# Row scores of the first attention as pairs of 64-row products, with queries and keys from float32r parts

## The reference, cut to what matters

```python
h = _layernorm(x, axis=-1) * (1 + ca) + sa
# _L0_attn_ref, H = 8 heads, R = 64 wide for queries and keys, values 128 wide
Q = (x @ Wq.T).reshape(b, n, H, R)
K = (x @ Wk.T).reshape(b, n, H, R)
V = (x @ Wv.T).reshape(b, n, H, d)
attn = jnp.einsum('bnhr,bmhr->bhnm', Q, K)
attn = jax.nn.softmax(attn, axis=-1)
out = jnp.einsum('bhnm,bmhd->bnd', attn, V)
```

## Time and profile before

| what | us |
|---|---|
| median of 3 runs | 3644.22 (3643.92 to 3647.78) |
| the profiled execution | 3644.25 |
| its span, first to last instruction | 3642.5 |
| attention, by the chain of its heads | about 35 to 1985 |
| TensorE busy in 1000 to 2000 us | 993.50 |
| VectorE busy in 1000 to 2000 us | 620.02 |
| ScalarE busy in 1000 to 2000 us | 491.84 |

### The profile page before, as it was taken

One profiled execution on the slowest core, in us unless ns is written; L12 is line 12 of the kernel. 1 busy time (PEld: TensorE's weight loads), 2 busy tenths in 40 slices (PEclk: granted clock), 3 DMA queues, 4 the chain that ended last, 5 costly groups with the idle time before them and its releaser, 6 DMA issues. The chain is left out here.

```text
span 3642.5 us, 82462 instructions
## 1 busy us (share of the span) xinstructions
PE 2897.9 (80%) x32284; PEld 2387.4 (66%) x32284; DVE 2611.7 (72%) x8488; ACT 1316.9 (36%) x2231; POOL 236.5 (6%) x155
## 2 busy tenths in 40 slices
PE   5999999999999999999999465656565666654455
PEld 2888888888888888888888344545454444442222
DVE  4565766756657566566664699999999999946775
ACT  2544454544444545454544022222222222211222
POOL 0000000000000000000000010000000000002220
PEclk9999999999999999999999666767676766766777
DMA  1000000000000000000000200000000000000000
GB/s 63 1 1 7 1 1 7 1 2 7 1 7 1 1 7 1 7 1 1 7 1 1 91 1 0 0 0 0 0 0 0 0 0 0 0 6 10 12 12 17
DMA packets 6415, 25.26 MB, mean 7 GB/s; under 512 B 1360, under 2 KB 1872, under 8 KB 5840
## 3 DMA queue, kind: packets, MB, share of 16 engines
q1 hardware_dynamic: 6224, 22.57, 1.6%
HBM read 14.18 MB, written 8.39 MB: 6 GB/s over the span
## 5 line engine op out<-in xcount | busy, mean ns | idle before, releaser
L605 PEld LDWEIGHTS obank<-v_one,probs 128*128 128x128 f32 x8192 | 1069.2, 190 | 91.1 <-issue 2.1
L605 PE MATMUL obank<-v_one,probs 128*128 128x129 f32 x8192 | 1078.6, 274 | 0.0
L352 ACT ACTIVATE probs<-bank 128x512 f32<-128x512 f32 x1024 | 583.8, 597 | 746.6 <-PE bank L593 450.2
L442 DVE TENSOR_REDUCE maxes<-ring 128x1 f32<-128x512 f32 x1024 | 659.7, 686 | 128.8 <-PE ring L573 105.6
L592 PE MATMUL bank<-q_hh,k_hl 128*128 128x512 f32 x1024 | 505.1, 493 | 1.6 <-issue 1.4
L593 PE MATMUL bank<-q_lm,k_h 65*128 65x512 f32 x1024 | 406.4, 397 | 0.0
L455 DVE RECIPROCAL recip<-obank 128x1 f32<-128x1 f32 x512 | 83.6, 163 | 414.2 <-PE obank L605 401.0
L573 PE MATMUL ring<-k_hl,q_hh 128*128 128x512 f32 x1024 | 338.4, 410 | 9.9 <-DVE k_hl L434 6.0
L1017 PE MATMUL ring<-ident_sb,to_turn 128*128 128x128 f32 x96 | 28.7, 437 | 365.7 <-ACT to_turn L855 359.7
L954 DVE TENSOR_TENSOR low_hot<-ids,low_iota 128x16384 f16<-128x16384 f16 x32 | 277.9, 8683 | 1.8 <-ACT ids L860 1.8
L1017 PEld LDWEIGHTS ring<-ident_sb,to_turn 128*128 128x128 f32 x96 | 16.1, 213 | 369.7 <-issue 340.3
(11 more groups left out here) (220 smaller groups left out, 3677.1 us busy)
## 6 DMA issues: line engine op xcount, KB each, us to landing
xt<-in_x SPq DMA_DIRECT2D x8, 512.0 KB, 8.6
out_x<-xt SPq DMA_DIRECT2D x8, 512.0 KB, 2.6
x<-out_x SPq DMA_DIRECT2D x1, 4096.0 KB, 12.0
out_x<-x SPq DMA_DIRECT2D x8, 512.0 KB, 2.6
pk_wq<-in_w_q SPq DMA_DIRECT2D x1, 1024.0 KB, 4.9
pk_wqT<-in_w_qT SPq DMA_DIRECT2D x1, 1024.0 KB, 7.1
wmod_sb<-in_wmod SPq DMA_DIRECT2D x2, 384.0 KB
w_qk_sb<-in_w_qk SPq DMA_DIRECT2D x1, 512.0 KB, 4.5
```

What stands on the lines that cost most here:

```text
L352: nc.scalar.activation(probs[:, half, i, :], st[s % 4], ACT.Exp).then_inc(st_free[s % 4], 1)
L442: nc.vector.tensor_reduce(maxes[:, i, k:k + 1], ring[bank_of(at)][:], AX.X, ALU.max).then_inc(rows_maxed, 1)
L605: mm = nc.tensor.matmul(obank[j % 2][:, 0:D + 1], probs[:, half, m, cols], v_one[h % 2][:, m, :], start=(m == 0), stop=(m == TB - 1))
```

## The change

It does three things.

1. Row scores. `k_top` is a new tile whose rows 64 to 127 hold the keys' float32r part. The product of key half 0 uses rows 0 to 63 of q_hh and k_hl; that of key half 1 uses rows 64 to 127 of q_hh and k_top. Both are 64-row products, on the two row halves of the array. The remainder of the keys is left out of the maxima (it stays in the scores that are exponentiated). Both banks are taken ahead of the first of the two.
2. ScalarE makes one more copy of 64x512 for each token half, into k_top, and VectorE and POOL wait for four copies instead of three.
3. Queries and keys come from three float32r products in place of a float32 one. The weights are split into two parts once; h is split for each batch by one more ScalarE copy and a VectorE subtraction for each half (`fine_h`, in slot 14 of head 6), and TensorE's q_and_k waits for that.

```diff
@@ ScalarE: turned_h and q_and_k
                 for k in range(2):
                     at = located(b, "t", ahead, k)
                     wait_full(b, at)
+                    nc.scalar.activation(hT_h[:, k * HALF:(k + 1) * HALF], ring[bank_of(at)][:], ACT.Copy).then_inc(hT_h_ready, 1)
                     nc.scalar.activation(hT[:, k * HALF:(k + 1) * HALF], ring[bank_of(at)][:], ACT.Copy).then_inc(hT_ready, 1)
...
                     nc.scalar.activation(q_hh[s][R:P, cols], bank[0:R, :], ACT.Copy).then_inc(hi_ready, 1)
+                    nc.scalar.activation(k_top[s][R:P, cols], bank[R:P, :], ACT.Copy).then_inc(hi_ready, 1)
@@ VectorE: q_and_k, the new fine_h, its place, and the start-up
-                    dve.wait_ge(hi_ready, 6 * g + 3 * k + 3)
+                    dve.wait_ge(hi_ready, 8 * g + 4 * k + 4)
...
+            def fine_h(b, ahead):
+                for k in range(2):
+                    cols = slice(k * HALF, (k + 1) * HALF)
+                    dve.wait_ge(hT_h_ready, 2 * (b + ahead) + k + 1)
+                    dve.wait_ge(hT_ready, 2 * (b + ahead) + k + 1)
+                    nc.vector.tensor_tensor(hT_l[:, cols], ring[bank_of(located(b, "t", ahead, k))][:], hT_h[:, cols].bitcast(F32), ALU.subtract).then_inc(hT_l_ready, 1)
...
+                        if s == 14 and h == H - 2 and not last:
+                            fine_h(b, 1)
...
+            link(nc.vector.tensor_copy(w_qk_h[:], w_qk_sb[:]))
+            nc.vector.tensor_tensor(w_qk_l[:], w_qk_sb[:], w_qk_h[:].bitcast(F32), ALU.subtract).then_inc(w_split, 1)
             dve.wait_ge(first_x_loaded, 16)
             for n in range(8):
                 first_norm(link, n, 0, 1)
+            fine_h(0, 0)
@@ TensorE: q_and_k and score_rows
-                pe.wait_ge(hT_ready, 2 * batch + 3)
+                pe.wait_ge(hT_l_ready, 2 * batch + 3)
                 for k in range(2):
                     at = located(b, "p", h, k)
-                    bank = take(b, at)
-                    give(at, nc.tensor.matmul(bank[:], w_qk_sb[:, h % H, :], hT[:, k * HALF:(k + 1) * HALF], start=True, stop=True))
+                    bank, cols = take(b, at), slice(k * HALF, (k + 1) * HALF)
+                    nc.tensor.matmul(bank[:], w_qk_l[:, h % H, :], hT_h[:, cols], start=True, stop=False)
+                    nc.tensor.matmul(bank[:], w_qk_h[:, h % H, :], hT_l[:, cols], start=False, stop=False)
+                    give(at, nc.tensor.matmul(bank[:], w_qk_h[:, h % H, :], hT_h[:, cols], start=False, stop=True))
...
-                for k in range(2):
-                    at = located(b, "a", h, i, k)
-                    bank = take(b, at)
-                    give(at, nc.tensor.matmul(bank[:], q_hh[s][:, i * P:(i + 1) * P], k_hl[s][:, k * HALF:(k + 1) * HALF], start=True, stop=True))
+                banks_ = [take(b, located(b, "a", h, i, k)) for k in range(2)]
+                for k, keys in enumerate((k_hl[s], k_top[s])):
+                    rows = slice(k * R, (k + 1) * R)
+                    give(located(b, "a", h, i, k),
+                         nc.tensor.matmul(banks_[k][:], q_hh[s][rows, i * P:(i + 1) * P], keys[rows, k * HALF:(k + 1) * HALF], start=True, stop=True))
```

More of the change, by code:

```diff
@@ L157, in build_attention @@
         k_hl = [sb(f"k_hl{i}", [P, N], F32R) for i in range(2)]
+        k_top = [sb(f"k_top{i}", [P, N], F32R) for i in range(2)]
+        w_qk_h = sb("w_qk_h", [P, H, 2 * R], F32R)
+        w_qk_l = sb("w_qk_l", [P, H, 2 * R], F32R)
+        hT_h = sb("hT_h", [P, N], F32R)
+        hT_l = sb("hT_l", [P, N], F32R)
         k_h1 = [sb(f"k_h1{i}", [R + 1, N], F32R) for i in range(2)]
@@ L174, in build_attention @@
         hT_ready = sem("hT_ready")
+        hT_h_ready = sem("hT_h_ready")
+        hT_l_ready = sem("hT_l_ready")
         ring_full = [sem(f"ring_full{r}") for r in range(2)]
@@ L190, in build_attention @@
         consts = sem("attn_consts")
+        w_split = sem("w_split")
         steps = sem("attn_steps")
         turns = sem("turns")
-        primed = [hT_ready, lo_ready, v_ready, rows_maxed, neg_ready, *st_free, *o_read]
+        primed = [hT_l_ready, lo_ready, v_ready, rows_maxed, neg_ready, *st_free, *o_read]
         def iteration_uses(b, h):
@@ L237, in released @@
             if kind == "t":
-                return hT_ready, shift(b, 2 * n + uses[at][2] + 1, 2)
+                return hT_l_ready, shift(b, 2 * n + uses[at][2] + 1, 2)
             if kind == "p":
@@ L285, in second_k @@
             def second_k(g, h):
-                pool.wait_ge(hi_ready, 6 * g + 6)
+                pool.wait_ge(hi_ready, 8 * g + 8)
                 if not (isinstance(g, int) and g < 2):
@@ L529, in _ @@
             pe.wait_ge(consts, 5)
+            pe.wait_ge(w_split, 1)
             def take(b, at):
@@ L550, in q_and_k @@
             def q_and_k(b, h, batch):
-                pe.wait_ge(hT_ready, 2 * batch + 3)
+                pe.wait_ge(hT_l_ready, 2 * batch + 3)
                 for k in range(2):
                     at = located(b, "p", h, k)
-                    bank = take(b, at)
-                    give(at, nc.tensor.matmul(bank[:], w_qk_sb[:, h % H, :], hT[:, k * HALF:(k + 1) * HALF], start=True, stop=True))
+                    bank, cols = take(b, at), slice(k * HALF, (k + 1) * HALF)
+                    nc.tensor.matmul(bank[:], w_qk_l[:, h % H, :], hT_h[:, cols], start=True, stop=False)
+                    nc.tensor.matmul(bank[:], w_qk_h[:, h % H, :], hT_l[:, cols], start=False, stop=False)
+                    give(at, nc.tensor.matmul(bank[:], w_qk_h[:, h % H, :], hT_h[:, cols], start=False, stop=True))
             def v_of(b, h):
+                pe.wait_ge(hT_ready, 2 * (b + h // H) + 2)
                 for k in range(2):
```

## The result

| kernel | median us | runs | profiled execution's span |
|---|---|---|---|
| before | 3644.68 | 4 (3643.92 to 3647.78) | 3642.5 |
| changed | 3823.73 | 4 (3820.5 to 3825.47) | 3823.5 |

The changed kernel is slower: its ratio to the kernel before is 1.0487, 95% interval 1.0472 to 1.0503, some 179 us. The forecast was 3800, range 3732 to 3858.

A forecast was written before the change was run, and what follows sets the result against it. TensorE's order of work was taken to set the pace, with a chain across three engines arriving together with it. Heads 135.5, h 9.9, start-up 9.0 and head 0's loop 1.5 add 155.9 to 3644.2: 3800 us, range 3732 to 3858.

The forecast's parts named there:

- The switches: Row-score slots on TensorE: two changes between 128 and 64 rows per slot, 0.20 us each, making the slot 2.00 us.
- The pair's overlap: Row scores on TensorE: the two 64-row products overlap, taking 0.235 us in place of 0.47.
- Both banks first: Row-score slots: the next pair waits until both banks are reduced, a second floor of 1.87 to 1.88 us, under 2.00.
- The chain: From q_and_k through ScalarE's copies and VectorE's subtractions to a head's first row scores: 1.23 - 0.15 - 0.06 = +1.02 us.
- The parts: q_and_k as float32r products: TensorE's time falls from 1.72 to 1.41 us, but TensorE then idles some 1.3 us.
- A head: One q_and_k to the next in attention: 1.02 + 1.17 - 0.04 = 2.15 us more, 63 times, 135.5 us.
- The split of h: Copies and subtractions of h once a batch delay q_and_k by 1.4 us, seven times: +9.9 us.
- The start-up: Before the regular heads: weights' split +2.6, h +1.4, q_and_k copies and products, row-score pairs +4.2; together +9.0 us.
- rival B: Row-score pair does not overlap, or only after the second weight load: 3853 or 3917 us; chance 0.15.
- The loop of head 0: Head 0's slots without products: maxima pairs go from 1.29 to 1.88 us, +1.5 us on top.
- A: Row-score slots: no switch cost, so waiting for both banks sets the slot at 1.88; 3735 us; chance 0.17.
- C: Faster: the extra waits are covered and only TensorE's time counts, about 3525 us; chance 0.05.

The follow-up runs named there:

- full rows: Changed kernel with 128-row products in place of the two 64-row ones (k_top still written, not read): 3783.67 us, ratio 1.0377.
- same half: Changed kernel with both 64-row products on rows 0 to 63: 4034.32 us, ratio 1.106; an earlier run of 9896.98 us was not used.
- the parts alone: Kernel before with only weights and h in two float32r parts and q_and_k as three products: 3648.18 us, ratio 1.0007.
- the copy alone: Kernel before with the extra ScalarE copy into k_top, never read, and VectorE and POOL waiting for it: 3725.36 us, ratio 1.0222.
- the banks one by one: Changed kernel with each ring bank taken directly ahead of its own 64-row product: 3804.22 us, ratio 1.0433.
- the last version: Kernel before with float32r parts, POOL making the queries' second copy, h copies in slot 13, weights split by ScalarE and POOL: 3618.86 us, ratio 0.9926.
- both banks first alone: Kernel before with both ring banks taken ahead of the two 128-row products of a tile: 3687.87 us, ratio 1.0115.
- padded kernel: Changed kernel with 128 always-met semaphore waits put ahead of TensorE's work: 3814.18 us, ratio 1.0462.

## Why the prediction held, and where it was short

- **The switches.** Forecast 0.20 us each and a slot of 2.00; measured 1.98, and 1.88 without them (full rows), where the banks' floor decides. The price of one switch follows from the same half against the parts alone, two streams of 512 columns a slot in both: (2.22 - 1.83) / 2, some 0.19 to 0.20. Right, from a stage of the kernel that the change does not touch. The Trainium skill's rule that a change of tiling mode drains TensorE (TensorEngine Tiling (Array Packing), Key Properties) holds here: 0.09 us pass between the end of the stream and the next load, and the load itself is no longer hidden.
- **The pair's overlap.** Forecast 0.235 us a slot; measured 2.22 - 1.98 = 0.24. Right.
- **Both banks first.** Forecast a second floor of 1.88, hidden behind the switches; measured 1.88 alone (1.94 in the first and the last batch) and no change of the steady slots when undone. Right.
- **The chain.** Forecast +1.02 us, measured 7.55 - 6.30 = +1.25. Two terms were mis-sized. The first bank was full only 0.08 sooner, not 0.15. And the load follows VectorE's release by 0.22 (1213.06 to 1213.28), where the sum had 0.07: the 0.13 of before (1015.14 to 1015.27) less 0.06. That 0.06 was not to be had: with the copy alone TensorE waits 1.11 us and its load still comes 0.12 after the release. The other 0.09 belongs to taking both banks first: the load comes 0.22 after the release in every kernel that does so, the kernel before with that one edit among them, and 0.12 in the changed kernel with the banks one by one, whose heads are no shorter. Alone, the copy costs 1.23 a head.
- **The parts.** Forecast: TensorE's 0.31 is lost in the wait. In the kernel before about half of it was lost (0.16 arrives); in the changed kernel TensorE waits 1.37 us, so the shorter products themselves gain nothing. With the chain taken out of the way, the last version gets more than 0.31 back, 0.46 a head, since the kernel before had a small wait of its own: its load came 6.30 after q_and_k and its first slot was 1.70 in place of 1.83.
- **A head**: forecast 2.15, measured 2.22. It is nearer than its terms: on the forecast's own footing they are 1.25 for the chain (forecast 1.02), 1.08 for the seven intervals (13.91 in place of 12.83; forecast 1.17) and -0.11 for the end (forecast -0.04), so an error of 0.23 met two of the other sign. That is in part luck. The split of h: 9.9 and 10.4. The start-up: 9.0 and 9.1. In rival B, 8 x 0.11 x 63 is 55 and not 54, which changes nothing.
- **The loop of head 0.** Forecast +1.5 beyond a regular head, measured +5.4. This step of the sum failed: pairs at 1.88 assumed full clock, and the clock was at half there, pairs at 2.23. Seven times 0.35 more is 2.4 us of the missing 3.9. TensorE had stood 3.97 us waiting for L444 up to the first pair:

```profile
97.00 0.76 PE L600 MATMUL ring<-k_hl,q_hh 64*128 64x512 f32 x1 [3.97 <-DVE k_hl L444]
...
100.00:110.00 10.00, 8.85 (x20) 3.76 (x18) 6.08 (x10) 2.39 (x4) 0.00 (x0) 0.50 0.01 2
```

The kernel before has a granted clock of 1.00 in this stretch, and 27.6 us for that loop. The loop is long too with both banks first alone (34.1) and with the banks one by one (34.9), and not with the copy alone (29.4) or the parts alone (27.8); which part of the change brings the clock down was not isolated, and the other 1.5 us are not traced. The start-up came out right because its forecast was made from rows that already had such slow products: 0.84 us from load to maxima against 0.53.

- **The loop's return.** Not in the sum at all: five heads at 37.4, where 32.45 and a regular head's 2.22 would be 34.67; 14 us. "The experts and the second layer are not touched" was right, but that five heads of the attention begin behind a branch, and can stall there, was left out. The padded kernel takes the 14 us away; their cause stays open, as said there.

The two missed terms and the 0.07 a head make up 22 of the 24 us by which 3800 was short. None of the rivals came true: A and B fall with full rows and same half, C with the two kernels in which the copy stands alone or is taken away.

## What to carry to other kernels

Two half-height products in place of two full ones save one stream, but each change between heights costs nearly a stream of 512 columns here: 0.20 against 0.235 us. A pair alone between neighbours of full height pays two switches, 0.40, to save 0.235. By these figures two pairs together would save 0.47 for the same 0.40; that is an estimate, and no run tried it. In the experts 512 such products stand together.

Ask of every instruction that is added to another engine whose wait it lengthens. A copy that nobody read cost 80 us in a kernel whose ScalarE was busy half the time, and making that same chain shorter than TensorE's own time was worth about 19 us, where the faster products alone were worth nothing.

## What was not expected of the hardware

- TensorE's stall at a loop's return changes with instructions that do nothing: 128 of them ahead of its work took the stalls of 1.14 and 2.11 us at the return shown above down to 0.66, and the half clock behind them away; the kernel was 9.5 us faster, with 14.5 us gone at the five returns and some come back elsewhere.
- With both 64-row products on one half, the granted clock between 1000 and 1800 us was 0.94 to 0.95, with TensorE busy 95% of that time, and the kernel 90 us slower than its slots explain. What the clock responded to stays open; no run tried it.
